# A graph network on one core: the dense part's keys made once and broadcast as one row a turn, the matrix zeroed in four transfers a turn

## The reference

```python
gathered = edge_val[:, None] * x[edge_col]
support = jax.ops.segment_sum(gathered, edge_row, num_segments=N)
h = jnp.concatenate([x, support], axis=1)
out = jax.nn.relu(h @ W + b)
...
x = _layernorm(x + _L0_gnn_ref(x, src, dst, edge_weight, L0_gnn_W, L0_gnn_b), axis=-1)
```

## Time and profile before

| | us |
|---|---|
| median of 3 runs | 7607.84 |
| lowest, highest | 7606.58, 7607.99 |
| profiled execution, its own time | 7607.18 |
| its span | 7605.5 |
| busy in the span: TensorE, VectorE, ScalarE, GpSimd | 5856.0, 3568.1, 1548.2, 5333.8 |

### The profile page before, as it was taken

One profiled execution on the slowest core, in us unless ns is written; L12 is line 12 of the kernel. 1 busy time (PEld: TensorE's weight loads), 2 busy tenths in 40 slices (PEclk: granted clock), 3 DMA queues, 4 the chain that ended last, 5 costly groups with the idle time before them and its releaser, 6 DMA issues. The chain is left out here.

```text
span 7605.5 us, 123237 instructions
## 1 busy us (share of the span) xinstructions
PE 5856.0 (77%) x30254; PEld 4311.3 (57%) x30254; DVE 3568.1 (47%) x14050; ACT 1548.2 (20%) x5117; POOL 5333.8 (70%) x5079
## 2 busy tenths in 40 slices
PE   3777777776628888867777766666699979998998
PEld 2444444445516555556666555555466656675665
DVE  4555655664436666645555533333222322323444
ACT  2333333331202222212222212222100000010001
POOL 3777777777647777657777577777577767776776
PEclk8888888887869999955555579988899999999999
DMA  8888888884224444323333234444477766766775
GB/s 276 192 173 164 167 156 165 168 157 117 84 77 117 116 117 116 103 71 79 82 80 80 69 110 118 118 118 118 151 230 233 237 190 225 236 222 208 246 241 178
DMA packets 680261, 1160.49 MB, mean 153 GB/s; under 512 B 137768, under 2 KB 440794, under 8 KB 671194
## 3 DMA queue, kind: packets, MB, share of 16 engines
q0 software_dynamic: 301456, 555.10, 32.7%
q1 hardware_dynamic: 376266, 575.81, 22.9%
q10 hardware_dynamic: 2304, 26.74, 0.8%
HBM read 912.88 MB, written 244.35 MB: 152 GB/s over the span
## 5 line engine op out<-in xcount | busy, mean ns | idle before, releaser
L898 POOL DMA_INDIRECT rows<-gcn_rows,index x1632 | 1549.4, 949 | 656.9 <-issue 460.4
L1432 POOL DMA_INDIRECT rows<-gat_rows,index x1568 | 1506.1, 961 | 657.3 <-issue 468.6
L1763 POOL DMA_INDIRECT support<-rows,index x784 | 1236.9, 1578 | 399.9 <-DMA support<-rows,index 225.8
L1563 PE MATMUL bank<-onehots,rows 128*128 128x128 f32 (+1 forms) x4704 | 947.2, 339 | 338.1 <-DVE rows L1639 337.9
L984 PEld LDWEIGHTS bank<-onehots,rows 128*128 128x128 f32 x6528 | 853.3, 193 | 418.8 <-issue 357.3
L1563 PEld LDWEIGHTS bank<-onehots,rows 128*128 128x128 f32 (+1 forms) x4704 | 720.9, 202 | 539.5 <-issue 323.7
L984 PE MATMUL bank<-onehots,rows 128*128 128x128 f32 x6528 | 880.9, 278 | 113.6 <-DVE onehots L1036 59.5
L674 POOL DMA_INDIRECT rows<-norm,index x784 | 742.8, 947 | 295.1 <-issue 283.2
L997 PE MATMUL dense_bank<-matrix,edge_space 128*128 128x512 f32 x1536 | 728.7, 597 | 0.0
L1872 PE MATMUL rows_bank<-x_window,cross 128*128 128x256 f32 x1568 | 626.8, 491 | 85.7 <-ACT cross L1856 84.6
L730 PE MATMUL bank<-onehots,rows 128*128 128x128 f32 x3136 | 486.8, 314 | 231.8 <-DVE onehots L761 207.3
(11 more groups left out here) (322 smaller groups left out, 8453.2 us busy)
## 6 DMA issues: line engine op xcount, KB each, us to landing
matrix<-matrix SPq DMA_DIRECT2D x96, 1024.0 KB
edge_space<-gcn_rows SPq DMA_DIRECT2D x138, 512.0 KB
alpha<-matrix SPq DMA_DIRECT2D x51, 1024.0 KB
dst_row<-in_dst_flat SPq DMA_DIRECT2D x100, 512.0 KB
source_row<-in_src_flat SPq DMA_DIRECT2D x99, 512.0 KB
matrix<-zeros SPq DMA_DIRECT2D x49, 1024.0 KB, 8.2
support<-zeros ACTq DMA_DIRECT2D x16, 1632.0 KB, 27.2
rows<-gcn_rows,index POOLq DMA_INDIRECT x1632, 4.7
```

The lines of the kernel that those rows point to most:

```text
L898: nc.gpsimd.indirect_dma_start(rows[:, k, :], None, table, bass.IndirectOffsetOnAxis(ap=index[:, k:k + 1], axis=0),).then_inc(gathered[k], 16)
L1432: nc.gpsimd.indirect_dma_start(rows[:, k, :], None, table, bass.IndirectOffsetOnAxis(ap=index[:, k:k + 1], axis=0),).then_inc(gathered[k], 16)
L1563: done = nc.tensor.matmul(to, left, onehots[:, k, :], start=first and c == 0, stop=final and c == chunks - 1)
L1763: nc.gpsimd.indirect_dma_start(support[k % COPIES], bass.IndirectOffsetOnAxis(ap=index[:, k // HALF, k % HALF:k % HALF + 1], axis=0), rows ...
```

## The change

The keys of the dense part's edges are made in `set_up` by one VectorE op, written to DRAM as one row of fp32 numbers (`key_row`), and broadcast to all partitions once a turn, in place of two int32 rows from which VectorE made the keys in each turn. The load goes into `tail_row` itself, so it waits until VectorE has finished with it at k = 13 of the turn before (`tail_used`). The matrix's zeros of a turn, 1 MB in one transfer of 8 KB a partition ahead of the turn's loads, go out in four transfers of 2 KB a partition, one behind each of the four loads. The padding that `lay_out` made for the two rows goes.

```diff
@@ scatter_by_source
-            tail_source, tail_dst = sbuf("tail_source", [P, width], INT32), sbuf("tail_dst", [P, width], INT32)
             tail_row = sbuf("tail_row", [P, width])
@@ SyncE, ahead of each turn's loads
                 def tail(i):
                     if not first_pass:
                         return
-                    piece = g.matrix.rearrange("(i p z) a -> p i (z a)", p=P, i=g.tiles // RING)[:, bass.ds(i, 1), :]
-                    sync.dma_start(piece.rearrange("p i z -> p (i z)"), zeros[:, 0:piece.shape[2]]
-                                   ).then_inc(g.matrix_zeroed, 16)
-
-                    sync.wait_ge(s.tail_keyed, i + 1)
-                    for tile, flat in ((tail_source, g.tail_source_flat), (tail_dst, g.tail_dst_flat)):
-                        sync.dma_start(tile[:], flat[0:1, bass.ds(i * (TAIL_BATCH * P), width)]
-                                       .to_broadcast([P, width])).then_inc(s.tail_loaded, 16)
+
+                    sync.wait_ge(s.tail_used, i + 1)
+                    sync.dma_start(tail_row[:], g.key_row[0:1, bass.ds(i * (TAIL_BATCH * P), width)]
+                                   .to_broadcast([P, width])).then_inc(s.tail_loaded, 16)
+
+                matrix_steps = g.matrix.rearrange("(i q p n) a -> p i q (n a)", i=g.tiles // RING, p=P, n=GROUP)
+
+                def zero(i, q):
+
+                    if first_pass:
+                        sync.dma_start(matrix_steps[:, bass.ds(i, 1), q, :].rearrange("p i n -> p (i n)"),
+                                       zeros[:, 0:GROUP]).then_inc(g.matrix_zeroed, 16)
@@ SyncE, the two halves of a turn
                         sync.wait_ge(s.multiplied, i * RING + HALF * (h + 1))
                         sync.dma_start(x_window[:, h, :], g.x_dram[bass.ds(base, P), :]).then_inc(x_loaded[h], 16)
+                        zero(i, 2 * h)
 
                         sync.wait_ge(s.matrices, i * RING + HALF * (h + 1))
                         sync.dma_start(
                             source_row[:, h, :, :].rearrange("p k e -> p (k e)"),
                             g.source_flat[0:1, bass.ds((i * 2 + h) * (HALF * P), HALF * P)]
                             .to_broadcast([P, HALF * P])).then_inc(row_loaded[h], 16)
+                        zero(i, 2 * h + 1)
@@ VectorE, tail_step(i, k)
-                    if k == 0:
-
-                        dve.wait_ge(s.tail_loaded, i * 32 + 32)
-                        nc.vector.scalar_tensor_tensor(tail_row[:], tail_source[:], KEY, tail_dst[:], ALU.mult, ALU.add
-                                                       ).then_inc(s.tail_keyed, 1)
                     v = k - 2
                     if 0 <= v < TAIL_BATCH:
                         if v == 0:
-                            dve.wait_ge(s.tail_keyed, i + 2)
+
+                            dve.wait_ge(s.tail_loaded, i * 16 + 16)
                             dve.wait_ge(s.gates_ready, i + 1)
...
                     if k == HALF + TAIL_BATCH:
                         dve.wait_ge(s.tail_own, i * TAIL_STEPS + 2 * TAIL_BATCH)
+                        dve.sem_inc(s.tail_used, 1)
...
                 if first_pass:
-                    dve.sem_inc(s.tail_keyed, 1)
+                    dve.sem_inc(s.tail_used, 1)
@@ set_up, SyncE
+                sync.wait_ge(s.keyed, 1)
+                lead = no_key.shape[1]
+                lane, at = divmod(g.turns * RING * P, g.tiles)
+                head = g.tiles - at
+                row = g.key_row[0]
+                sync.dma_start(row[0:lead].unsqueeze(0), no_key[:]).then_inc(s.keys_kept, 16)
+                sync.dma_start(row[lead:lead + head].unsqueeze(0), chunk_key[lane:lane + 1, at:]).then_inc(s.keys_kept, 16)
+                sync.dma_start(row[lead + head:lead + head + (P - 1 - lane) * g.tiles].rearrange("(p n) -> p n", n=g.tiles),
+                               chunk_key[lane + 1:, :]).then_inc(s.keys_kept, 16)
+                sync.dma_start(row[g.key_row.shape[1] - P:].unsqueeze(0), no_key[:, 0:P]).then_inc(s.keys_kept, 16)
+                sync.wait_ge(s.keys_kept, 64)
@@ set_up, VectorE
+                nc.vector.memset(no_key[:], -1.0)
+                nc.vector.scalar_tensor_tensor(chunk_key[:], g.source_chunk[:, 0:g.tiles], KEY, chunk_dst[:], ALU.mult,
+                                               ALU.add).then_inc(s.keyed, 1)
@@ build_program
-    g.tail_source_flat, g.tail_dst_flat = t.src_tail, t.dst_tail
+    g.key_row = dram("key_row", [1, (tiles - g.tail + 2) * P])
...
-                    pool.wait_ge(g.matrix_zeroed, 16 * (tiles // RING))
+                    pool.wait_ge(g.matrix_zeroed, 16 * GROUPS * g.rows)
```

More of the change, by code:

```diff
@@ L58, in dense_sizes @@
     g.tail = g.tiles - g.tiles // RING * TAIL_BATCH
+    assert GROUPS * g.rows == 4 * (g.tiles // RING)
     g.untouched = math.ceil(g.first_dense / P) + 3
@@ L1737, in scatter_by_source @@
                    "issued", "matrices", "crossed", "cross_copied", "multiplied", "rows_ready", "counted",
-                   "values_ready", "tail_loaded", "tail_keyed", "tail_own", "gates_copied", "gates_ready", "gates_used", *names) as (block, s):
+                   "values_ready", "tail_loaded", "tail_used", "tail_own", "gates_copied", "gates_ready", "gates_used", *names) as (block, s):
             scattered = s[-HALF:]
@@ L2107, in set_up @@
         chunk_before = sbuf("chunk_before", [P, g.tiles], INT32)
+        chunk_key, no_key = sbuf("chunk_key", [P, g.tiles]), sbuf("no_key", [1, (g.turns * RING - g.tail + 1) * P])
         attribute = sbuf("attribute", [P, g.tiles])
@@ L2125, in set_up @@
         with phase(nc, "loaded", "iota", "own", "relu", "added", "gated", "kept",
-                   "turned", "wide", "zeros_ready") as (block, s):
+                   "turned", "wide", "zeros_ready", "keyed", "keys_kept") as (block, s):
             @block.sync
@@ L3555, in pad @@
         return whole[:tiles * P]
-    def tail(a, value):
-        around = np.full((tiles - g.tail + 2) * P, value, a.dtype)
-        first = g.turns * RING
-        around[(first - g.tail + 1) * P:(tiles - g.tail + 1) * P] = a[first * P:]
-        return around.reshape(1, -1)
     def by_tile(a):
@@ L3572, in lay_out @@
     dst_flat = np.concatenate([dst, np.full(2 * HALF * P, nodes, dst.dtype)])
-    arrays.update(x=x, src_flat=src.reshape(1, -1), dst_flat=dst_flat.reshape(1, -1), src_tail=tail(src, 0),
-                  dst_tail=tail(dst, nodes + 1), src_tile=by_tile(src), src_chunk=src.reshape(P, tiles), dst_tile=by_tile(dst),
+    arrays.update(x=x, src_flat=src.reshape(1, -1), dst_flat=dst_flat.reshape(1, -1), src_tile=by_tile(src), src_chunk=src.reshape(P, tiles), dst_tile=by_tile(dst),
                   dst_chunk=dst.reshape(P, tiles), before_chunk=before.reshape(P, tiles),
```

## The result

The changed kernel took 7565.83 us (median of 5 runs, 7553.65 to 7571.42) against 7606.58 of the kernel before (median of 5). The ratio is 0.9951, 95% interval 0.9938 to 0.9963: some 37 us faster, where 105 had been forecast. The profiled execution took 7571.42 us. A turn is 16 scatters, counted from 0 as in the code, so scatter 9 is the tenth. In what follows "waits" is GpSimd's idle time in the scatter loop less 784 x 0.30 and less the wait for the first scatter; "lengthened issues" is its busy time less 784 x 1.54; "the loop" runs from the first scatter's start to the last one's end.

A forecast was written before the change was run, and what follows sets the result against it. Bound: GpSimd's scatter pace plus waits from DMA congestion behind one large group. Surplus of 3.55 us a turn becomes 0.7 + 0.7 = 1.4, gaining 2.15 x 49 = 105 us: 7607 - 105 = 7502 us, forecast range 7473 to 7541, wider range 7450 to 7585.

The forecast's parts named there:

- The bound and the place: Scatter loop: GpSimd's pace bounds it, with a surplus of 173.6 us from DMA congestion behind one large group of SyncE's transfers.
- The failed step: Waits behind SyncE's two groups: drain times of 7.5 and 5.4 us against 5.5 us free leave 0.7 us a turn.
- The linear reading: GpSimd's waits: only 640 KB of a group is free, slope 2.9 / 1920 KB; the two groups cost 2.2 us a turn.
- rival A: Scatter loop: the stall only splits over both groups, surplus 2.8 us a turn, gain 37 us, 7570 us; chance 12%.
- Short packets: Zeros in the scatter loop: packets four times shorter hold up scatters less, so waits taken nearer the low end, 0.7 us.
- Rival C: Scatter loop: short packets alone let scatters keep pace, no wait left, surplus 0.4 us a turn, 7453 us; chance 15%.
- Lengthened issues: GpSimd's scatter issues beside SyncE's groups: 0.6 us a turn becomes 0.7, bounds 0.3 and 1.2.
- The wait that moves: SyncE's row load waits for k = 13; VectorE starts scrap some 4.3 us late (L = 9.3), at cost 0.
- Rival D: VectorE's loop: late source_row[0] becomes the bound from L = 13.6 us; at 14.9 the kernel takes 7671 us; chance 7%.
- Rival B: DMA engines: total DMA work bounds, so no change that can be told, 7605 us; chance 5%.
- rival E: SyncE's queue: each piece of zeros holds it 2.3 us instead of 1.2, surplus 4.0 us a turn, 7629 us; chance 3%.
- Setting up: Before the scatter loop: making and writing the keys hides under other waits, cost 0, upper bound 5 us.

The follow-up runs named there:

- the key row alone: The changed kernel with the zeros of a turn put back into one transfer of 1024 KB; 7545.04 us, ratio 0.9932, and 0.9925 when run again.
- the run with 8 KB runs: The changed kernel with each piece of zeros written from 32 partitions with 8 KB each instead of 128 with 2 KB; ratio 0.9969.
- the run with the row loaded second: The changed kernel with the load of the key row moved behind the first half's loads of the turn; ratio 0.9981.
- the paced run: The changed kernel with the four pieces of zeros issued by GpSimd's count of scatters, meant to stand outside SyncE's groups; ratio 0.9856.

## Why the prediction was wrong

**The bound and the place** were right: GpSimd's pace in the scatter loop, waits behind SyncE's groups, 1616.2 us with 173.6 of surplus. With the zeros away from the groups (ahead of the loop, or late in one transfer) it came to 1481 to 1489 us.

**The failed step** is "Past the free 5.5 us the first leaves 2.0 x 1.06 / 2.9 = 0.7 us of wait and the second none", with "I take 0.7". The waits measured are 119.4 / 49 = 2.4 us a turn, against 2.9 before: 85 us more than the sum had. Even without the first 12 turns, the first group, 1600 KB, costs 1.22 us, and the second, 1152 KB, which by my drain rate ends inside the free time, costs 0.71. I had fitted a rate, a latency and a free time to one group of one size, and the fit reproduced that size (2.4 for 2.9) without having been held against a smaller one. The loop's gain is then 105 - 85 + 25 (the issues, below) = 45 us, against 45.7 measured; the profiled execution lost 10 of it outside the loop.

The linear reading that I gave as the upper bound (2.2 us) was the better one. It is rival A, at 12% and 7570 us, with "waits of 1.5 us behind both groups"; measured are 1.2 and 0.7. Taken from the same 37 turns before (2.52 us for 1920 KB above 640), the line gives 1.26 and 0.67. That it fits so well is in part luck: it would charge the key row alone 0.59 us for its group of 1088 KB, which costs 0.03, and groups of 1152 KB cost 0.53 to 1.19 from kernel to kernel. A's 7570 for 7566 is luck too: more waits, fewer lengthened issues and 10 us lost outside the loop cancel.

**Why the split gave nothing.** The zeros' 1024 KB cost 1.7 to 1.8 us a turn when they stand in the groups, in one transfer or in four: 111.6 - 30.8 = 81 us for one, 119.4 - 30.8 = 89 for four. With the key row alone the group with the zeros holds 1664 KB and the other, 1088 KB, is free. The four pieces take 512 KB out of the one and put 512 into the other, which then costs 1.22. The gain in waits came from the row alone: it takes 896 KB out of the large group and puts 448 into the other, which stays free.

**Short packets.** I took the low end of the waits because the zeros' packets are four times shorter. If the effect exists it is some 22 us, a quarter of the 85 that were missing. Rival C (no wait is left) is refuted with it. The 12.9 us of factor, my evidence, show a transfer that waits beside 26.7 MB of another queue; they do not tell short packets from much traffic. The rule of the Trainium skill behind it ("DMA: Bandwidth & Descriptors", Queues, rings and completion order: the engines alternate between queue rows packet by packet) agrees in sign with the run with 8 KB runs, and what that run shows is nowhere near enough to free the scatters.

**Lengthened issues.** I took 0.7 us a turn; it is 8.8 / 49 = 0.18. Here the change did better than forecast, by 25 us, which hid part of the error in the waits. They vanish with the second int row: 27.3 us with the zeros in four and two rows, 7.3 with one row and one transfer, and 7.4 with one row right behind the other four, where SyncE issues five transfers nearly as close together as before. The tail_dst issue was the one that took 2.09 us on SyncE.

**The wait that moves** was right but for a little: VectorE's wait for source_row came to 264.4 us, 5.4 a turn (forecast 3 to 5), the wait for scatters fell from 372.7 to 155.8 as forecast, and the scrap op began 8.7 us after k = 13 in the mean of 46 turns (L forecast 9.3). Rival D needed 13.6. In the run with the row loaded second this lateness falls by more than half and GpSimd gains nothing.

**Rival B** (total DMA load) fell with the paced run, **rival E** (a fixed cost for each transfer) too: four paced transfers wait far less than one in a group. The run with the zeros ahead of the loop shows it without any scatters beside them; from 110 to 200 us of its trace:

```profile
q1 hardware_dynamic: 5287, 38.47, 101.2%
...
matrix<-zeros SPq DMA_DIRECT2D x33, 1024.0 KB, 25.8
```

38.47 MB in 90 us is 427 GB/s, or 2.5 us for each transfer of 1024 KB, though it landed 25.8 us after its issue (the median). The fit of 2.0 us that the prediction takes from the Trainium skill ("DMA: Bandwidth & Descriptors", Anatomy of one DMA) is given there for transfers that GpSimd issues; these are SyncE's, and 2.5 us each leave no room for 2.0 of their own.

**Setting up** moved the first scatter by 0.8 us in one profile (bound 5) and by 1.5 in another; the key row alone had it 1.1 us earlier.

**What stays open:** why 512 KB of zeros beside x_window and source_row cost 0.7 us when 1024 KB alone cost 0.2, why reads in their place cost nearly nothing in the second group and nearly as much in the first, and why the same 1152 KB cost 0.71 us in one kernel and 1.19 in another. Whether source_row's broadcast from one row of DRAM is the partner that matters was not tried.

## What to carry to other kernels

A transfer that nobody waits for still costs when it goes out beside ones that are waited for: place it by the progress of the engine that its congestion would stop, not behind the loads that happen to share its queue. Then look in the trace where it really went out; two of the placements here were not where I had put them. Splitting by itself gained nothing: inside the groups the four pieces waited as much as the one (119.4 and 111.6 us), and outside them one transfer waited less than two or four (40.0, 51.2 and 52.3), because a piece of each had not left a group. A fit of rate and free time to one burst size must be held against a second size before it forecasts a third; until then, the straight line through the two sizes that the trace does show is the better guess, and no more than a guess.

## What the runs showed of the hardware

A scatter that was issued while SyncE issued four transfers of 1152 KB together, with a row of 448 KB 1.6 us ahead of them, landed in about 8 us, where about 4 is usual (4.1 at most in the turn shown before): 1064.70, waited for until 1073.35. A lone transfer of 1024 KB did next to nothing (0.2 us a turn). GpSimd's issues were longer (1.98 us in the mean of the scatter beside the large group, 1.92 with the zeros in four, instead of 1.54) only in the kernels in which SyncE issued two int rows behind the other loads; five transfers within 2.6 us, one row among them, did not lengthen them. Transfers of 1024 KB issued one behind the other, with nothing beside them, drained at 427 GB/s.
